# Attention with quantized probabilities: row maxima computed one query block ahead, integer keys kept resident, score tiles waiting in pairs

## The reference

```python
q = ((layernorm(x) @ Wq + bq) * 0.25)      # 1600 queries, 16 heads of 16
k, v = split(ctx @ Wkv + bkv)              # 23104 keys, shared by all queries
q = fq_sym(q, axis=-1)                     # per row: round(x / s) * s, s = max|x| / 127
k = fq_sym(k, axis=-1)
v = fq_sym(v, axis=keys)
attn = softmax(q @ k.T)                    # per head, over 23104 keys
attn = fq_unsigned(attn, axis=-1)          # round(attn / s) * s, s = max(attn) / 255
x = x + (attn @ v) @ Wp + bp
x = x + moe_ffn(layernorm(x))              # 8 experts with low-rank updates, top 2
```

## Time and profile before

| | |
|---|---|
| median of 3 runs | 8783.29 us (8783.18 to 8784.29) |
| profiled execution | 8781.1 us, span 8779.3 us |
| PE / DVE / ACT / POOL busy | 8199.8 / 6555.9 / 5411.7 / 5197.0 us |
| mean granted clock of PE | 0.957 |
| chain that ended last | PE 85%, DVE 6%, issue 4%, POOL 2% |

### The profile page before, as it was taken

One profiled execution on the slowest core, in us unless ns is written; L12 is line 12 of the kernel. 1 busy time (PEld: TensorE's weight loads), 2 busy tenths in 40 slices (PEclk: granted clock), 3 DMA queues, 4 the chain that ended last, 5 costly groups with the idle time before them and its releaser, 6 DMA issues.

```text
span 8779.3 us, 223739 instructions
## 1 busy us (share of the span) xinstructions
PE 8199.8 (93%) x60312; PEld 2566.9 (29%) x60312; DVE 6555.9 (75%) x6161; ACT 5411.7 (62%) x12138; POOL 5197.0 (59%) x3573
## 2 busy tenths in 40 slices
PE   8954999999999999999999999999999999988688
PEld 4510222222222222222222222222222222222343
DVE  8989777777777777777777777778777777720466
ACT  2300676767676767676767676767667676777333
POOL 5743565656565656565656565656656565666356
PEclk9955999999999999999999999999999999999799
DMA  5663011010102020202020202010111101020000
GB/s 164 209 159 100 14 25 21 18 28 18 28 12 34 11 35 12 34 12 34 12 34 12 34 12 34 12 30 17 26 20 25 21 18 28 18 42 7 10 4 4
DMA packets 305414, 303.94 MB, mean 35 GB/s; under 512 B 50718, under 2 KB 297802, under 8 KB 300458
## 3 DMA queue, kind: packets, MB, share of 16 engines
q1 hardware_dynamic: 304682, 303.13, 15.9%
q10 hardware_dynamic: 672, 0.16, 0.0%
HBM read 226.31 MB, written 76.71 MB: 35 GB/s over the span
## 4 chain that ended last, share of the span: by engine, by line
PE 85%; DVE 6%; issue 4%; POOL 2%; ACT 1%; DMA 1%; DVEq 0%; SPq 0%; ACTq 0%; POOLq 0%
PE psum L1397 31%; PE psum L1366 26%; PE psum L1324 16%; PE psum L1376 6%; DVE mpart L1187 3%; PE psum L1289 2%; ACT y L1086 1%; POOL mix L393 1%; PE psum L655 1%; PE psum L1358 1%; DVE act_c L534 1%; PE psum L1424 1%; POOL kq L935 1%; POOL kq L928 0%; PE psum L628 0%
## 5 line engine op out<-in xcount | busy, mean ns | idle before, releaser
L1187 DVE TENSOR_REDUCE mpart<-psum 128x978 f32 x4992 | 5654.4, 1171 | 1416.6 <-PE psum L1324 1343.9
L1086 ACT ACTIVATE y<-psum 128x400 f32<-128x400 f32 x11520 | 5007.1, 506 | 2063.8 <-PE psum L1397 1971.3
L1006 POOL TENSOR_SCALAR xh<-y 128x1600 f16<-128x1600 f32 x2880 | 4391.4, 1525 | 2754.6 <-PE psum L1376 1550.7
L1397 PE MATMUL psum<-QT,K 99*128 x11520 | 3180.4, 341 | 68.3 <-ACT y L1086 55.7
L1366 PE MATMUL psum<-y,ones 128*17 128x400 f32 x23048 | 2540.2, 508 | 0.0
L1324 PE MATMUL psum<-K,QS 48*128 48x489 bf16 x9984 | 1769.3, 391 | 225.6 <-DVE mpart L1187 184.0
L1397 PEld LDWEIGHTS psum<-QT,K 99*128 x11520 | 876.7, 97 | 2616.7 <-issue 2475.2
L1376 PE MATMUL psum<-xh,vwin 128*16 128x400 f16 x11528 | 1019.6, 335 | 0.7 <-POOL xh L1006 0.7
L1324 PEld LDWEIGHTS psum<-K,QS 48*128 48x128 bf16 x9984 | 433.9, 94 | 1489.0 <-issue 1017.0
L1366 PEld LDWEIGHTS psum<-y,ones 128*17 128x17 f32 x23048 | 402.8, 96 | 652.1 <-issue 651.7
L1376 PEld LDWEIGHTS psum<-xh,vwin 128*16 128x16 f16 x11528 | 323.0, 90 | 624.2 <-issue 397.3
(11 more groups left out here) (180 smaller groups left out, 2145.9 us busy)
## 6 DMA issues: line engine op xcount, KB each, us to landing
K<-kT_parts SPq DMA_DIRECT2D x204, 240.0 KB, 8.3
vwin<-v_int SPq DMA_DIRECT2D x579, 80.0 KB, 1.9
K<-kT_parts SPq DMA_DIRECT2D x772, 45.8 KB
kT_parts<-part SPq DMA_DIRECT2D x135, 256.0 KB, 3.2
K<-kT_parts SPq DMA_DIRECT2D x102, 242.0 KB, 8.4
src<-in_ctx_dram SPq DMA_DIRECT2D x46, 512.0 KB, 4.5
v_float<-kv SPq DMA_DIRECT2D x45, 512.0 KB, 5.2
vin<-v_float SPq DMA_DIRECT2D x9, 2560.0 KB, 10.2
```

What stands on the lines that cost most here:

```text
L1006: pool.tensor_scalar(xh[:, g % YR, :, :], y[:, g % YR, :, :], INT_STEP, 0.0, ALU.mult, ALU.add)\
L1086: act.activation(y[:, s % YR, j, :], s2_bank(GT * s + j), ACT.Exp).then_inc(exp_done, 1)
L1187: dve.tensor_reduce(mpart[:, t, ds(2 * cp + j, 1)], s1_buf(n)[:, :, 0:CHALF], AX.XY, ALU.max)\
L1397: pe.matmul(s2_bank(t), K3[0:MROW, h % 2, ds(c * REGION + t * P, P)], queries, start=True, stop=True).then_inc(s2_ready, 1)
```

## The change

**One block ahead.** A block's 400 queries are cut into 3 full tiles of 128 and a rest of 16; the rests of the 4 blocks of a head make one more tile (QX, with keys in K1X), computed over the head. A block computes the maxima of the block that follows it: 72 jobs and 6 of the rest tile, 78 as before. 7 of them are the "lead", the first jobs of the block after next, computed in the last body. The bodies have 27, 27 and 24 jobs (JOBS_AT, SPLIT, LATE). The prologue computes only 4 x 24 jobs for the first block and 7 for the lead; the last head now has jobs too (for a block that nobody reads). Maxima, transpose and copy come once a block, in the third body: DVE's part at the start of group 10, the transpose and ACT's copy at group 12. SP then brings the rows into QT with three transfers, with six at the end of a head.

**Resident keys.** All integer keys of a head for one half lie in K1 (two halves on two groups of partitions), loaded in three pieces; chunks are overlapping windows of 489 columns, 481 apart.

**Score tiles.** K3 holds one head, not two; its regions are loaded anew behind the last block. All three bodies are written out, so key addresses are constants. Tiles 0 and 1 share one wait, and so do 2 and 3.

**Prologue.** Values pass through three input and two output buffers; v_float is stored so that four rows lie side by side. The rounding of the last rest (vox) comes behind all chunks, and POOL's list of constants behind that.

```diff
-CHUNKS = 2 * BODIES
-CSTEP = 962
-CSIZE = NK - (CHUNKS - 1) * CSTEP
-CHALF = CSIZE // 2
-JOBS = 2 * QT_TILES
+CHUNKS = 24
+HALF = NK // 2
+CHALF = 489
+CSTEP = (HALF - CHALF) // (CHUNKS - 1)
...
+PAIRS = (0, 2)
+PT = 3
+LEAD = 7
+N_JOBS = (27, 27, 17 + LEAD)
+ROUND_AT = (5, 7, 9, 11, 13, 15, 17, 19, 21)
+MAX_AT, TURN_AT = 10, 12
...
         def bodies(eng, body, head_start=...):
-            with eng.Fori(0, H - 1) as h:
-                head_start(h, True)
-                with eng.Fori(0, BLOCKS) as b:
-                    body(h, b, 0, True)
-                    with eng.Fori(1, BODY_C) as c:
-                        body(h, b, c, True, later=True)
-                body(h, None, None, True)
...
+            with eng.Fori(0, H) as h:
+                head_start(h)
+                with eng.Fori(0, BLOCKS) as b:
+                    for c in range(BODY_C):
+                        body(h, b, c)
...
 # PE, a score tile
-                        pe.wait_ge(exp_done, T + t + 1)
-                        pe.matmul(s2_bank(t), K3[0:MROW, h % 2, ds(c * REGION + t * P, P)], queries,
+                        if j in PAIRS:
+                            pe.wait_ge(exp_done, T + t + 2)
+                        elif j - 1 not in PAIRS:
+                            pe.wait_ge(exp_done, T + t + 1)
+                        pe.matmul(s2_bank(t), K3[0:MROW, c * REGION + t * P:c * REGION + (t + 1) * P], queries,
...
 # PE, the groups of a body
+                    if c == BODY_C - 1 and s == TURN_AT:
+                        maxima(B + 1, at, done, job_buf(c, done))
+                        extra = 2
                     score_tile(s, 0)
                     score_tile(s, 1)
-                    next_jobs(1 if s in SPLIT else JOBS_AT[s])
+                    if s not in LATE[c]:
+                        next_jobs(1 if s in SPLIT[c] else JOBS_AT[c][s])
                     score_tile(s, 2)
                     score_tile(s, 3)
-                    if s in SPLIT:
+                    if s in SPLIT[c] or s in LATE[c]:
                         next_jobs(1)
...
 # SP, behind q == 1 of the third body
+                            after_job(at + OWN - 1)
+                            load_tiles(QS, h, b, 2, turn, qs_in)
+                            sp.wait_ge(mt_copied, block_of(h, b) + 2)
+                            load_m((h + (1 if end else 0)) % 3, 0 if end else b + 1)
+                            if end:
+                                load_m_tail((h + 1) % 3)
```

More of the change, by code:

```diff
@@ L740, in load_q @@
             def load_q(head, ring):
                 for row, i in QROWS:
[L742 to L750 removed]
+                    queries = QT[row:row + HD, ring, :].rearrange("d (b r) -> d b r", b=BLOCKS)
@@ L831, in load_ffn @@
+            for r in range(1, BODY_C):
+                load_region(0, r)
+            sp.wait_ge(q_in, 192)
+            load_q(1, 1)
             def load_ffn(part):
@@ L882, in _ @@
-            for piece in range(2):
-                sp.wait_ge(qs_in[piece], 96 * (H + 1))
+                with sp.Fori(0, 2) as b:
+                    block(h, b, False)
+                for b in range(2, BLOCKS):
+                    block(h, b, False, b)
+            with sp.Fori(0, 2) as b:
+                block(H - 1, b, True)
+            for b in range(2, BLOCKS):
+                block(H - 1, b, True, b)
+            for piece in range(3):
+                sp.wait_ge(k1_in[piece], 32 * (H + 1))
@@ L1074, in body @@
                 for s in range(GROUPS):
-                    if not later and s == LAG_PV:
+                    if c == 0 and s == LAG_PV:
                         act.wait_ge(summed, YR + groups_before(h, b, 0))
@@ L1095, in _ @@
         def _(dve):
[L1097 removed]
+            dve.wait_ge(x_in, 32 * BLOCKS)
             dve.wait_ge(zeroed, 9)
@@ L1312, in _, with job @@
             last.then_inc(qi_turned, 1)
-            def job(head, cp, t, j, at, n, first=False):
-                if t == 0:
-                    pe.wait_ge(k1_in[j], 32 * (BODIES * head + cp + 1))
-                for piece in range(2):
-                    if first and j == 0 and t == QS_PARTS[piece][0]:
-                        pe.wait_ge(qs_in[piece], 96 * (head + 1))
+            def job(tile, keys, at, n, buf):
                 pe.wait_ge(s1_free, at + n + 1)
@@ L1344, in _ @@
             pe.sem_inc(pv_done, YR - LAG_PV)
-            with pe.Fori(0, BODIES) as cp:
-                for n in range(JOBS):
-                    job(0, cp, n % QT_TILES, n // QT_TILES, JOBS * cp, n, first=True)
-            maxima(0, PRO_SLOTS - 2)
+            pe.wait_ge(qs_in, 32)
+            pe.wait_ge(qx_in, 32)
+            for chunk in range(CHUNKS):
+                if piece_of(chunk) >= 0:
+                    pe.wait_ge(k1_in[piece_of(chunk)], 32)
+                for t in range(PT + 1):
+                    n = (PT + 1) * chunk + t
+                    job(tile_of(t, False), key_window(K1, chunk), 0, n, s1_buf(n))
+            maxima(0, 0, 4 * CHUNKS, s1_buf(4 * CHUNKS))
+            pe.wait_ge(ql_in, 32)
+            for n in range(4 * CHUNKS + 2, PRO_SLOTS):
+                i = n - 4 * CHUNKS - 2
+                job(tile_of(i % PT, True), key_window(K1, i // PT), 0, n, s1_buf(n))
             pe.wait_ge(ones_ready, 2)
@@ L1401, in next_jobs @@
                     nonlocal done
-                    for _ in range(count if pass1 else 0):
-                        job(h + 1, BODY_C * b + c, done % QT_TILES, done // QT_TILES, at, done + extra, not later)
+                    for _ in range(count):
+                        t, chunk, lead = job_of(c, done)
+                        if t == PT:
+                            if c == 0 and chunk == 0:
+                                pe.wait_ge(qx_in, 32 * (h + 2))
+                            pe.wait_ge(k1x_in[chunk], 32 * (body_of(h, b, c) + 1))
+                            keys = K1X[:, chunk, :]
+                        else:
+                            keys = key_window(K1, chunk)
+                            if c == 0 and done == 0:
+                                pe.wait_ge(qs_in, 32 * (B + 2))
+                            if lead and done == OWN:
+                                pe.wait_ge(ql_in, 32 * (B + 2))
+                            if t == 0 and piece_of(chunk) >= 0:
+                                pe.wait_ge(k1_in[piece_of(chunk)], 32 * ((B + (2 if lead else 1)) // BLOCKS + 1))
+                        job(tile_of(t, lead), keys, at, done + extra, job_buf(c, done + extra))
```

535 lines of the change are left out of this document (306 added, 229 removed).

## The result

The changed kernel takes 8991.7 us (median of 4 runs, 8988.6 to 8994.0), the kernel before 8783.2: ratio 1.0237, 95% interval 1.0221 to 1.0254. It is 208 us slower, where 8626 was predicted. The profiled execution took 8990.0 us for a span of 8988.1.

A forecast was written before the change was run, and what follows sets the result against it. DVE was taken to bound the prologue's maxima and PE the scores stage. From a span of 8779.3 us, 201 less for the prologue and 44 more for the PE stage gave 8622, plus 4 made 8626 us; range 8540 to 8700.

The forecast's parts named there:

- the 2.3 us above plus 0.4: Change of block on PE: 2.3 us as before plus 0.4 for registers, less 0.2 for DVE waits; 2.5 us taken.
- S: PE group of four score tiles with one maxima job: 2.36 us forecast, 2.32 before.
- P: PE group with two maxima jobs, one of them behind tile 3: 2.67 us forecast, 2.64 before.
- D: PE group with two maxima jobs together: no loss from shared waits, all take 2.38 us.
- tile 2 at +0.94: Under the shared wait, score tile 2 starts 0.94 us into the group, 0.06 behind tile 0's exponential.
- the middle body: Second of a block's three bodies on PE, 27 jobs: 37.1 us forecast.
- the handover: Maxima rows passed to the next block's scores: expected to fit, by 1.2 us where tightest.
- The transpose and copy: Once a block, in the third body: between nothing and 1 us, 0.4 us taken.
- Handover rows late: Rival: each block pauses for its maxima rows and PE's clock drops, 397 us, 9020 in all; chance 0.08.
- Score waits cost nothing: Rival: tile 2 never late, S and P groups 0.18 us shorter in 26 groups, 300 us, 8325; chance 0.08.
- The prologue: Stage ahead of the scores: PE stage starts at 680 instead of 881.3 us, 201 us less.
- Transfers were taken as the bound: Prologue: about 40 MB at 258 GB/s end at 653.5, DVE alone at 639.4; 652 taken.

The follow-up runs named there:

- f0: Changed kernel with all 64 blocks written out on PE and ACT, and ACT's two older waits on an instruction of their own; 8616.3 us, ratio 0.9812.
- e1: Changed kernel with the four blocks of a head written out on PE and ACT; 8734.5 us.
- f1: Changed kernel, 64 blocks written out on PE and ACT, waits unshared, ACT's older waits on their own instruction, POOL's constants early, feed-forward loads in last head; 8336.4 us.
- p2: Changed kernel, 64 blocks written out on PE and ACT, POOL's constants early, first values asked for only after the first keys land; 8816.7 us.
- e2: Changed kernel with the four blocks of a head written out on PE alone, ACT still branching at each block; 8803.0 us.

## Why the prediction was wrong

**The step that failed** is the seam of the block, "the 2.3 us above plus 0.4", taken as 2.5 us. It priced the seam from waits, transposes and register work, all of which were there in the kernel before. What the change does to the code itself, writing out three bodies where a loop over one had served, was used only to make addresses constant. It takes PE's loop past what stays loaded, and each seam pays 3.0 us of standing still and about 2.5 us of low clock behind it: 119.24 against 113.57 to 113.75, so 5.5 us a block, some 350 us in all. The terms for waits, transposes and registers held (f0); the term for the longer code was missing. Without it, and with ACT's waits in order, the same kernel takes 8616 (f0): the forecast was 8626, though in that a stage that starts 41 us late (721.4) and 64 blocks that are 0.7 us shorter (113.57, 44 us in all) cancel by luck.

The Trainium skill, "Runtime: NRT & Kernel Launch", section "Instruction fetch mechanics", says that a taken branch whose target is outside the current window of two pages must wait for a fetch of the target's page. In kind the trace agrees (3.57 us a branch, 10 packets a block). In size it does not: the section's pages hold 256 instructions, and a loop of 1,531 rows branched back in 0.21 us without a fetch. The section also gives PE room for 2,048 instructions; here a loop of 1,663 was already fetched anew. The measurement decides in both.

**Right:** S 2.35 and P 2.66 to 2.67 (2.36 and 2.67), D 2.38, tile 2 at +0.94, the matmul of tile 3 at +1.12, the middle body 37.0 us (37.1), the last part 616.5, and the handover: in e1 no pause is left at a block's start. The transpose and copy cost 0.33 us at group 12 in the changed kernel (0.4).

**The rivals.** "Handover rows late" had nearly the time (9020) and a pause of nearly the right length, but it named the wrong mechanism. "Score waits cost nothing" priced waits that hold nobody up at 0.18 us in 26 groups, 300 us; unshared waits are worth 4.1 us a block, 262 us (f0 against f1). The prediction was right that the change does not have them free; it did not say that the change gives them away by sharing.

**The prologue** was 45 us too short, in three terms. The first job ran at 532.4, not 510.5: the store of q_int and the wait behind it held the loads until 506.9 (498.5 taken), and the keys then shared the DMA engines with 2.6 MB of values (without these beside them, in p2, the first reduce came 7 us earlier). DVE's stretch from the first reduce (533.1) to the last rounding (694.8) was 161.7 us, not the 141.5 that lie between 510.5 and 652. Transfers were taken as the bound there and DVE's own work as 128.9 us, and the bound was DVE after all, held up by POOL. The roundings show it, before and after (line, count, ns smallest/median/largest):

```profile
L1215 DVE TENSOR_SCALAR vo<-vin x9: 2816/2819/2819, 532.0 to 779.2; 128x5120 f16<-128x5120 f32 x9
```

```profile
L1320 DVE TENSOR_SCALAR vo<-vin x9: 2810/4915/13570, 559.1 to 683.4; 128x5120 f16<-128x5120 f32 x9
```

Before, no rounding met a multiply of POOL. After, seven of nine did, and each of the seven ended 2.7 us behind the end of POOL's multiply, whenever it had begun. One pair, and the rounding after it with POOL idle (start, length):

```profile
661.21 10.96 POOL L1058 TENSOR_TENSOR vin<-vin,vinv 128x5120 f32<-128x5120 f32 x1 [7.75 <-DMA vin<-v_float]
```

```profile
665.11 9.74 DVE L1320 TENSOR_SCALAR vo<-vin 128x5120 f16<-128x5120 f32 x1 [0.30 <-DMA v_int<-vo]
...
683.44 2.81 DVE L1320 TENSOR_SCALAR vo<-vin 128x5120 f16<-128x5120 f32 x1
```

POOL ends at 672.2, the rounding at 674.9. The other way round, a multiply of POOL that met a rounding took 13.5 us instead of 11.0. So here the two did not slow each other down but took turns; DVE's reduces beside POOL kept their 1.09 us. The roundings lost 30.4 us by it in sum; with DVE's 128.9 and 2.5 us of idle time that makes 161.8. POOL's list was 28 us bare, as predicted; the start came 2 us behind it. The transfers did not set the end. (The formula quoted ahead of the result from "DMA: Bandwidth & Descriptors" of the Trainium skill stands in the section "Anatomy of one DMA", not under "Measured", and is a fit for one transfer of GpSimd's. The busiest 40 us here moved 287 GB/s.)

## What to carry to other kernels

Before unrolling a loop on an engine, count the instructions from branch to branch and look at the duration of the branch row and at the packets of the instruction queues: a loop that fits costs 0.2 us a turn, one that doesn't 3 us and the low clock behind it, and then it was better here to write out far more (no branch) than a little more. A wait shared by two instructions is the later one's: count what the earlier one gives away. When a bare list is moved under other work, look for the wait that comes next. When two engines are set to work on the same stretch, look whether each one's instructions keep their length.

## What the runs showed of the hardware

PE's loop code stayed loaded at 1,555 rows and was fetched anew every turn at 1,663 and more; the branch then took 3.4 to 4.7 us (medians) instead of 0.21. ACT's own branch row stays at 0.045 us, and its first row behind it came 2.6 us later in the changed kernel. After a pause of 3.0 us PE ran 6.6 us at half clock; where only ACT held it up (e2), a seam cost 1.4 us and the block's mean clock stayed 1.00. A rounding on DVE (2.82 us) that met a two-input multiply on POOL (10.96 us) ended 2.7 us behind the multiply's end, seven times of seven. With constants ACT's last wait became an instruction of its own and the exponential started 0.08 us later; with another instruction ahead to carry the older waits it did not.
